# MLP and query/key products in three float32r passes, a longer loop body, and a reordered step in two of five passes of a vision kernel

## What is computed

```
L0: x + fc2(gelu(conv1d_3(fc1(layernorm(x)))))       # a scan direction is picked per image
L1: y = x + proj(attention_7x7(layernorm(x)));  y + fc2(gelu(fc1(layernorm(y))))   # hidden 384
L2: x + proj(attention_7x7(n, bias, mask) + depthwise_conv7x7(n)),  n = layernorm(x)
L3: y = x + proj(attention_7x7(layernorm(x)));  y + fc2(gelu(fc1(layernorm(y))))   # hidden 384
```

## Time and profile before

| what | value |
|---|---|
| median of 3 runs | 12328.4 us (12321.03 to 12351.76) |
| the profiled execution's own time | 12346.31 us |
| its span, first to last instruction | 12344.5 us |
| mean granted PE clock | 0.978 |
| PE busy | 11557.4 us, 94% of the span |
| ACT, DVE busy | 7537.9 and 7030.2 us, 61% and 57% |
| POOL busy | 1543.8 us, 13% |

### The profile page before, as it was taken

The page is one execution under the profiler, slowest core; times in us unless marked ns, Lnnn a source line. Parts: engine busy times, 40 slices in busy tenths (PEclk is TensorE's granted clock), DMA queues, the critical chain, the costliest instruction groups (busy, mean ns, idle before and its releaser), DMA issues. The chain is left out here.

```text
span 12344.5 us, 381409 instructions
## 1 busy us (share of the span) xinstructions
PE 11557.4 (94%) x153876; PEld 7528.1 (61%) x153876; DVE 7030.2 (57%) x12108; ACT 7537.9 (61%) x12498; POOL 1543.8 (13%) x2308
## 2 busy tenths in 40 slices
PE   6999998899999999999998999998999999999999
PEld 3434443566666666666675667666666666666666
DVE  4444444556556555555446666666555555555555
ACT  4555554566566566566435777776666666666666
POOL 0000000222222222222000000000111111111111
PEclk9999999899999999999999999999999999999999
DMA  1111111122222222222463333333000000000000
GB/s 56 37 36 39 40 39 34 37 46 46 45 45 46 46 44 47 44 47 45 153 216 69 76 75 76 75 75 66 21 21 21 21 21 21 22 21 21 22 21 20
DMA packets 1104420, 602.40 MB, mean 49 GB/s; under 512 B 864651, under 2 KB 1076566, under 8 KB 1099704
## 3 DMA queue, kind: packets, MB, share of 16 engines
q1 hardware_dynamic: 1091496, 553.66, 19.0%
q10 hardware_dynamic: 12288, 38.54, 0.9%
HBM read 308.38 MB, written 282.75 MB: 48 GB/s over the span
## 5 line engine op out<-in xcount | busy, mean ns | idle before, releaser
L950 PEld LDWEIGHTS banks<-L_ident,L_PR 113*113 113x113 f32 x9216 | 1104.5, 180 | 415.6 <-issue 290.1
L1264 DVE COPY L_VB<-banks 49x384 f32<-49x384 f32 x512 | 287.3, 561 | 1859.4 <-PE banks L966 1859.4
L1026 PE MATMUL banks<-L_XN,L_W 97*128 97x392 f32 x3072 | 1249.0, 516 | 13.2 <-DVE L_XN L1339 0.7
L1185 ACT ACTIVATE L_PR<-L_SX 113x588 f32<-113x588 f32 x1536 | 1084.3, 706 | 277.0 <-DVE L_SX L1301 270.5
L950 PE MATMUL banks<-L_ident,L_PR 113*113 113x113 f32 x9216 | 1249.1, 272 | 2.5 <-ACT L_PR L1185 1.8
L1295 DVE TENSOR_REDUCE L_MX<-banks 113x12 f32<-113x588 f32 x1024 | 783.4, 765 | 605.3 <-PE banks L988 605.3
L1169 ACT COPY L_PT<-banks 113x452 f32<-113x452 f32 x1792 | 871.1, 528 | 395.3 <-PE banks L950 395.2
L378 PE MATMUL banks<-scan_XS,scan_W1T 97*96 (+1 forms) x2688 | 1110.2, 551 | 0.0
L1103 PE MATMUL banks<-L_Hd,L_W 128*97 128x392 f32 x3072 | 1097.2, 493 | 0.0
L1005 PE MATMUL banks<-L_VB,L_PT 113*49 113x34 f32 x36864 | 1074.0, 214 | 2.5 <-ACT L_PT L1169 1.0
L1005 PEld LDWEIGHTS banks<-L_VB,L_PT 113*49 113x49 f32 x36864 | 1026.1, 127 | 26.9 <-issue 1.3
(11 more groups left out here) (199 smaller groups left out, 20433.5 us busy)
## 6 DMA issues: line engine op xcount, KB each, us to landing
L_X<-after_L SPq DMA_DIRECT2D x768, 147.0 KB
after_L<-L_X SPq DMA_DIRECT2D x512, 147.0 KB
conv_T<-L_norm_by_phase SPq DMA_DIRECT2D x96, 512.0 KB, 3.3
L_norm_by_phase<-L_XP SPq DMA_DIRECT2D x512, 84.0 KB, 2.2
scan_XT<-in_x SPq DMA_DIRECT2D x33, 1176.0 KB, 7.0
L_norm<-L_XA SPq DMA_DIRECT2D x256, 147.0 KB, 2.0
L_conv<-conv_D ACTq DMA_DIRECT2D x96, 392.0 KB, 3.0
L_XR<-L_norm SPq DMA_DIRECT2D x256, 147.0 KB, 2.2
```

Source lines behind the costliest of these rows:

```text
L950: mm = pe.transpose(bank(TURN[a])[0:SPAN, (k % 4) * SPAN:(k % 4 + 1) * SPAN], PR[:, st.v if lag else st.u, 2 * k:2 * k + 2, :].rearrange(" ...
L1026: pe.matmul(bank((7, 6, 7)[j])[:, 0:CH], W1[0:C + 1, j * 128:(j + 1) * 128], XN2[:, st.u], start=True, stop=True).then_inc(s[f"fc1_{j}"], 1)
L1185: act.activation(PR[:, u, a, 0:TOK], SX[:, u, a], ACT.Exp).then_inc(s[f"probs{half}"], 1)
```

## The change

In L1 and L3, keys, queries, the hidden blocks and fc2 become three float32r products each, with high and low parts. The weights are split once, ahead of the pass. XN and the three GELU outputs are split by POOL (two instructions each), XN2 by ACT (high) and DVE (low). fc2 and the residual X2 move one step later (chunk t-3); L1's third norm moves to stage `o` (chunk t-4). On PE the queries follow the keys at once into bank 3, and fc2 stands in the first part of the step. On DVE the copy of turned probabilities `pt_copy(st, 0)` and X2 stand first, then the keys; values follow the norms. SQ2 goes from POOL to ACT. The loop body of all three window passes holds 24 steps (10 rounds) after 14 steps written out.

```diff
-FIRST = 6
+FIRST = 14
+UNROLLED = 24
...
-    with eng.Fori(0, (NCH - 2 - FIRST) // 4) as i:
-        for j in range(4):
-            step(Step(eng, sems, i * 4 + (FIRST + j), FIRST + j, False))
+    with eng.Fori(0, (NCH - 2 - FIRST) // UNROLLED) as i:
+        for j in range(UNROLLED):
+            step(Step(eng, sems, i * UNROLLED + (FIRST + j), FIRST + j, False))
...
+            split_weights(nc, kind + "_parts", [(t[0:C + 1], h[0:C + 1], l[0:C + 1]) for t, h, l in ((Wq, WqH, WqL), (Wk, WkH, WkL), (W1, W1H, W1L))]
+                          + [(W2[:], W2H[:], W2L[:])])
...
+                def by_parts(out, wh, wl, xh, xl):
+
+                    for n, (wt, xt) in enumerate(((wh, xh), (wh, xl), (wl, xh))):
+                        mm = pe.matmul(out, wt.bitcast(F32R), xt.bitcast(F32R), start=(n == 0), stop=(n == 2))
+                    return mm
...
+                def output(st, j):
+
+                    st.wait(f"hd_parts_{j}", 3)
+                    for n, (wt, xt) in enumerate(((W2H, HdH), (W2H, HdL), (W2L, HdH))):
+                        mm = pe.matmul(bank(6)[0:C + 1, 0:CH], wt[:, j, :].bitcast(F32R), xt[:, st.v, j].bitcast(F32R),
+                                       start=(j == 0 and n == 0), stop=(j == HB - 1 and n == 2))
+                    return mm
...
                     if st.f:
 
-                        st.wait("xn", 0)
+                        st.wait("xn_parts", 0)
+
+                        st.wait("gelu_2", 3)
                         keys(st)
+
+                        st.wait("v_even", 1)
+                        st.wait("v_odd", 1)
+                        queries(st)
+                    if st.n:
+
+                        st.wait("gelu_1", 3)
+                        output(st, 0)
+                        output(st, 1)
                     if st.k:
                         st.wait("probs0", 1)
                         turn(st, 0)
...
+                    if st.n:
+                        output(st, 2).then_inc(s["fc2"], 1)
...
                     if st.m:
-                        st.wait("xn2", 2)
+                        st.wait("xn2_parts", 2)
...
-                    if st.m:
-                        for j in range(HB):
...
+                        st.wait("xn2", 2)
+                        act.copy(XN2H[:, st.u].bitcast(F32R), XN2[:, st.u]).then_inc(s["xn2_high"], 1)
...
+                        act.activation(SQ2[:, st.v], x1_of(st, 1)[0:C], ACT.Square).then_inc(s["sq2"], 1)
...
+                    if st.m:
+
+                        st.wait("xn2_high", 2)
+                        dve.tensor_tensor(XN2L[:, st.u].bitcast(F32R), XN2[:, st.u], XN2H[:, st.u], ALU.subtract).then_inc(s["xn2_parts"], 1)
...
+                    def split_rows(st):
+
+                        held(st, "xn", 0)
+                        pool.tensor_copy(XNH[:, st.u].bitcast(F32R), XN[:, st.u]).then_inc(s["xn_high"], 1)
+                        held(st, "xn_high", 0)
+                        pool.tensor_tensor(XNL[:, st.u].bitcast(F32R), XN[:, st.u], XNH[:, st.u], ALU.subtract).then_inc(s["xn_parts"], 1)
```

More of the change, by code:

```diff
@@ L140, in _, with split_weights @@
                     pe.matmul(ps[0:C + 1, 0:1], bias_row, one, start=True, stop=True).then_inc(column_ready, 1)
+def split_weights(nc, name, parts):
+    with semaphores(nc, name) as sem:
+        rounded = sem("rounded")
+        with nc.Block() as block:
+            @block.vector
+            def _(dve):
+                for whole, high, low in parts:
+                    dve.tensor_copy(high.bitcast(F32R), whole).then_inc(rounded, 1)
+                dve.wait_ge(rounded, len(parts))
+                for whole, high, low in parts:
+                    dve.tensor_tensor(low.bitcast(F32R), whole, high, ALU.subtract)
 def load_all(nc, name, pairs, zeros=(), ones=(), values=()):
@@ L917, in norms @@
                     nx = st.ahead()
-                    return ([(0, SQ[:, nx.u])] if nx.f else []) + ([(1, SQ2[:, st.u])] if st.m else []) + ([(2, SQ3[:, st.v])] if st.n and kind == "L1" else [])
+                    return ([(0, SQ[:, nx.u])] if nx.f else []) + ([(1, SQ2[:, st.u])] if st.m else []) + ([(2, SQ3[:, st.u])] if third_norm(st) else [])
                 def variances(st):
@@ L981, in scores @@
                             st.wait("xn", -1)
-                        if st.n:
-                            st.wait("xh" if kind == "L1" else "y", 3)
+                        if third_norm(st):
+                            st.wait("xh", 4)
+                        if kind == "L3" and st.n:
+                            st.wait("y", 3)
                     for q in range(NWIN):
@@ L1153, in rstd @@
                 def rstd(st):
-                    present = [g for g, there in enumerate((st.ahead().f, st.m, st.n and kind == "L1")) if there]
+                    present = [g for g, there in enumerate((st.ahead().f, st.m, third_norm(st))) if there]
                     whole = present == list(range(len(present)))
@@ L1216, in mlp_step @@
                         probs(st, 0, 0)
+                    if st.k:
+                        st.wait("variances", 0)
+                        st.wait("x1", 1)
+                        act.activation(SQ2[:, st.v], x1_of(st, 1)[0:C], ACT.Square).then_inc(s["sq2"], 1)
+                    if st.f:
                         probs(st, 1, 0)
@@ L1413, in step @@
                         if st.n and kind == "L1":
-                            c = st.t - 5
+                            st.wait("variances", 0)
+                            held(st, "x2", 3)
+                            pool.tensor_tensor(SQ3[:, st.v], X2[0:C, st.v], X2[0:C, st.v], ALU.mult).then_inc(s["sq3"], 1)
+                        if st.ahead().f:
+                            split_rows(st.ahead())
+                        if third_norm(st):
+                            c = st.t - 6
                             if not st.static or c >= 0:
-                                pool.wait_ge(norm_stored[st.v], (c // 2 + 1) * 16)
@@ L1429, in step @@
                             ins.then_inc(s["xp"], 1)
[L1430 to L1434 removed]
+                        if st.m:
+                            split_units(st, 0, 2)
+                            split_units(st, 1, 2)
                     square_rows(Step(pool, s, 0, 0, True), 0)
```

155 lines of the change are left out of this document (83 added, 72 removed).

## The result

The kernel after takes 11911.5 us (median of 3 runs, 11907.6 to 11917.8) where the kernel before takes 12328.4: ratio 0.966, interval 0.964 to 0.968. It is 3.4% faster; forecast were 5.7% and a range that ends at 11900. The sign was right, and 287 us of the gain are missing.

What follows compares the result with a forecast made beforehand. PE's own row of work was taken to bound L1 and L3, the loop second, in L1 alone; 12346 - 323 (L1) - 274 (L3) - 127 (loops) + 20 (small parts) = 11642, against the median 11625 us; range 11430 to 11900.

Steps and rivals of the forecast that it cites:

- Float32r products: PE in L1 and L3: three float32r products 0.54 us for 0.66, eight products a step giving 0.96 us.
- L1's two waits: PE's waits for POOL's SQ3 and ACT's RS both go: 0.57 us a step in L1, 0.27 in L3.
- The first rival: Float32r products on PE cost 0.23 us whatever the columns: 504 us back, 12130 us; chance 0.10.
- the better case: Float32r at the column bound: L3's steps at 12.8 us, L1's at 12.2, 11470 us in all; chance 0.12.
- the ring is 10.1: L3: the dependency cycle through POOL takes 10.1 us, so PE's row of 13.04 rules; step taken as 13.2.
- L1's step: L1: ring over POOL of 11.8 us, PE's row 12.13, step taken as 12.4; 323 us saved.
- the rival's (0.20) contention: L1: DVE's XN2L and POOL's copy of XN hold each other up, about 0.5 us; step 12.9, 11750 us; chance 0.20.
- one of the prediction's own signs of being wrong: The prediction is wrong if XN2L on DVE or its neighbours last longer than 0.55 us.
- Loops: Branches back: L1 loses 230 us, 27 remaining branches at 3.8 cost 103 in all three passes; net -127 us.
- nothing in L2 and L3: Bound on the branch cost: none in L2 and L3, as before; the other bound was twice 3.8 us.
- Small parts: Splitting the weights on DVE +10 us, one more stage to drain in L1 +10 us.
- the slower case: POOL writes float32r at a higher price than float32; at a factor of 2, 13490 us; chance 0.05.

Runs made afterwards that it cites:

- the mended version: Kernel after, with ACT's wait on hd_parts_2 moved in front of XN2's high part and XN's high part copied by ACT instead of POOL; 11607.3 us, ratio 0.940.
- padded: Kernel after, with 100 semaphore increments in front of everything on PE, DVE, ACT and POOL; 11861.9 us, ratio 0.960.

## Why the prediction was wrong, point by point

- **Float32r products** at 0.54 for 0.66, and **L1's two waits**: right in the net, in part by luck. Both waits are gone, and L3 without its table-load wait runs at 13.07 for the 13.04 of PE's row. But by starts in L3 the eight products took 5.64 us before and 4.92 in the mended version, 0.72 less and not 0.96, since the starts at either end of a group stand 0.22 to 0.29 apart where those inside stand 0.18; some 0.2 came from the transposes and the projection beside them, which the sum didn't have. The first rival (0.23 whatever the columns) and the better case (0.163) fall.
- **The step that failed in L3** (0.56 of 13.2, 143 us, half of the shortfall): "In L3 XA and XP are missing, the ring is 10.1 and PE rules". POOL doesn't rule there, as said, but a ring that I hadn't drawn does: hidden block, table load (1.28), GELU output 0, four operations on POOL, the second fc2 term. I had counted ACT's share as one copy and overlooked what a second wait in front of `gelu_0` does to the load. Moving that wait takes L3 to PE's row.
- **L1's step** (0.22 of 12.4, 56 us): a ring over POOL rules, as said, but not the one drawn. It closes at the second fc2 term, with output 1; the last term, which the prediction let output 2 release, waits for nothing. From one second term to the next (3011.41 to 3024.08) it takes 5.70 us to the copy of XN, over PE's row and DVE's X2, KX and norms, 2.07 for XN's parts (forecast 1.53), 1.46 for XA and XP, and 3.44 for GELU outputs 0 and 1: 12.67 for 11.8, of which the 0.6 allowed for hand-offs covered most. Mis-sized were POOL's subtraction, 1.02 for 0.84 (priced by a square, which reads one tile), three times in this ring, and the copy of XN, 0.88 for 0.54. The last is the rival's (0.20) contention, at 0.36 for the 0.5 supposed, and it is POOL that is held; a neighbour of XN2L above 0.55 was one of the prediction's own signs of being wrong. Independently, the table load closes L1 at 12.62.
- **Loops** (107 us): "nine branches remain that cost what L1's do: 27 x 3.8 = 103 us". For the code of before the sum was right to 3 us (106), by luck, as 2.7, 6.1 and 2.9 average to 3.9. The changed code pays 210: PE stops twice, 5 us together in L1, and part of a step is at 1.2 GHz. Of the 7.8 us a branch, 2.4 go with the place of the code in the kernel after (5.4 on average once padded). The 1.5 between that and 3.9 lie in L1 and L3, where PE passes the branch itself in 0.29 us with the steps of before and stands 3.5 us or more with the changed ones, and where the clock is then down at each branch. Why PE has to stand there stays open. The other engines stand too, but inside PE's time. The bound "nothing in L2 and L3" fell, "twice 3.8" held on average.
- **Not in the sum**: L2's even steps of 8.03 us held a cost of the short body, 0.17 each, 43 us.
- **Small parts** +20: the account's 3 us left over speak for it; no run takes it apart. **Float32r on POOL** (the slower case): the type costs nothing. **No change**: the run with no branch back ends it, as code fetched in line stalls nothing. Its price was also added up wrongly: 1.2 us on 512 steps are 614, which makes 12240 us and not 12330.

One wait moved and one copy on another engine bring 11607 us, inside the range and 18 us from the forecast. That closeness is luck: branches that cost 118 us more than forecast stand against steps that cost 105 less than the allowances (0.28 in L1, 0.13 in L3) and L2's 43. With no branch back the kernel takes 11364 us, 8.0% under the kernel before (ratio 0.920).

## What to carry to other kernels

Draw a ring through every engine that the new code's data crosses, with table loads in it, before saying that PE rules, and close it at each place where PE waits, not at the last alone; and where a repair of one wait brings nothing, try it beside the repair of the next, because two rings can be equally long. Give a wait of ACT that can stand earlier to an instruction ahead of a table load, so that the load itself waits for nothing late. Price an operation by a row that reads as many tiles, and a loop's branch by the body as it will be: L3's four steps of before, which stay loaded, cost nothing at the branch, the same four with more instructions 4.8 us each time.

## What the runs showed of the hardware

- With two waits in front of the first GELU, the compiled program put the late one ahead of its table load: 1.28 us then stood behind the wait, 512 times.
- POOL, 392 columns: 0.80 us with one tile read, 0.97 with two, 0.46 for a copy; float32r as float32, 96 partitions as 128.
- A DVE subtraction of two SBUF tiles stood for 7.92 us while POOL worked without a gap, and the next took 0.55. The other way round, POOL's cast took 0.88 us beside such a subtraction and 0.51 without.
- The same code cost 6.1 or 8.3 us a branch in L2, by where it lay. In L1 of the kernel after every engine stood 2.6 to 4.2 us at a branch (medians), at the same time; with four steps in the body PE alone did, and the branch cost as much.
- While PE stood for 3.65 us, and again for 1.32, its granted clock was down to 0.50 (1.2 GHz), from 2681 to 2689, and it was 1.00 again from 2692.
